# Attention stage of a fused attention and recurrent-thought kernel: VectorE normalises the results and adds five of eight causal masks, and a group's work is put in a new order

## The reference, cut to what matters

```python
xn = layernorm(x)
q, k, v = rope(xn @ wq.T), rope(xn @ wk.T), xn @ wv.T      # four query heads share one key/value head
scores = einsum(q, k) / sqrt(32) + causal_mask
attn = softmax(scores)
s = einsum(attn, v) @ wo.T
thought = layer_norm(xn)[:, -1, :] @ agg_w + agg_b
for _ in range(4):
    t = gelu(layer_norm(thought) @ d1_w + d1_b)
    thought = thought + (t @ d2_w + d2_b)
g = silu(layer_norm(xn + sigmoid(xn @ gate_w + gate_b) * (thought @ bc_w + bc_b)))
out = x + s * g
```

## Time and profile before

| | |
|---|---|
| median of 3 runs | 2551.06 us (2550.72 to 2552.27) |
| profiled execution, its own time | 2551.3 us |
| its span | 2549.6 us |
| PE busy | 2477.5 us, 97% |
| DVE busy | 1687.1 us, 66% |
| POOL busy | 1368.7 us, 54% |
| ACT busy | 981.7 us, 39% |

### The profile page before, as it was taken

How to read it: one execution, slowest core, us unless ns; L and a number is a source line. 1 busy time by engine, 2 the same in 40 slices (tenths; PEclk the granted TensorE clock), 3 DMA queues, 4 the chain that set the end, 5 groups by cost and what they waited for, 6 DMA issues and landing times. The chain is left out here.

```text
span 2549.6 us, 43562 instructions
## 1 busy us (share of the span) xinstructions
PE 2477.5 (97%) x14180; PEld 1679.2 (66%) x14180; DVE 1687.1 (66%) x3459; ACT 981.7 (39%) x1649; POOL 1368.7 (54%) x641
## 2 busy tenths in 40 slices
PE   5999999998999999999999999999899999999998
PEld 4888888885555555555555555555478888888886
DVE  5445554544777776777677777777477777777777
ACT  2111111110666665666666666666511111111111
POOL 0122212113999999999999999999511111111111
PEclk9999999997999999999999999999999999999999
DMA  6444454556755665556556656654666666655666
GB/s 247 178 151 150 161 184 175 187 172 225 208 179 168 194 207 171 179 192 205 158 189 202 181 167 195 207 176 142 237 138 124 123 123 123 123 116 114 116 117 121
DMA packets 228018, 428.90 MB, mean 168 GB/s; under 512 B 16837, under 2 KB 99781, under 8 KB 227929
## 3 DMA queue, kind: packets, MB, share of 16 engines
q1 hardware_dynamic: 154536, 375.85, 44.7%
q0 software_dynamic: 73392, 51.91, 13.9%
HBM read 313.67 MB, written 113.51 MB: 168 GB/s over the span
## 5 line engine op out<-in xcount | busy, mean ns | idle before, releaser
L961 DVE CUSTOM_DVE_ANT_0 bcast<-mxp,mask_q 128x128 f32<-128x128 f32 (+7 forms) x1024 | 726.4, 753 | 308.1 <-PE mxp L1073 175.1
L879 ACT ACTIVATE pr<-stp 128x512 f32<-128x512 f32 x1152 | 649.4, 595 | 447.3 <-PE stp L1082 332.2
L823 POOL TENSOR_TENSOR acc<-acc,pr 128x2048 f32<-128x2048 f32 x96 | 440.9, 4593 | 4.4 <-POOL acc L823 3.8
L1454 PE MATMUL gp<-g,shared 128*128 128x512 f32 x1536 | 356.1, 391 | 10.9 <-DVE g L1392 8.2
L1454 PEld LDWEIGHTS gp<-g,shared 128*128 128x128 f32 x1536 | 290.0, 189 | 72.0 <-DVE g L1392 8.5
L1454 PE MATMUL op<-o,shared 128*128 128x512 f32 x1280 | 311.2, 389 | 3.2 <-DVE shared L1442 3.2
L1094 PE MATMUL yp<-pr,vs 128*32 128x512 f32 (+3 forms) x3088 | 306.8, 492 | 0.0
L1454 PEld LDWEIGHTS op<-o,shared 128*128 128x128 f32 x1280 | 240.2, 188 | 53.9 <-DVE shared L1442 4.0
L322 POOL TENSOR_TENSOR r<-rt,r 128x1024 fp32r<-128x1024 f32 x40 | 95.9, 2397 | 279.7 <-ACT r L357 279.7
L1082 PE MATMUL stp<-qs,shared 97*128 97x512 f32 x576 | 238.6, 453 | 3.3 <-ACT pr L879 2.7
L1082 PE MATMUL stp<-shared 97*128 97x512 f32 x576 | 238.7, 452 | 0.0
(11 more groups left out here) (169 smaller groups left out, 3574.9 us busy)
## 6 DMA issues: line engine op xcount, KB each, us to landing
wch<-in_d_w SPq DMA_DIRECT2D x132, 1024.0 KB, 9.7
shared<-xt_scratch POOLq DMA_DIRECT2D x66, 512.0 KB, 6.3
q_scratch<-r SPq DMA_DIRECT2D x64, 512.0 KB, 3.6
shared<-q_scratch SPq DMA_DIRECT2D x96, 256.0 KB, 8.2
qs<-q_scratch SPq DMA_DIRECT2D x96, 256.0 KB, 7.9
yr<-y_scratch POOLq DMA_DIRECT2D x33, 512.0 KB, 5.9
xs<-in_x SPq DMA_DIRECT2D x33, 512.0 KB, 5.5
y_scratch<-ys SPq DMA_DIRECT2D x65, 256.0 KB, 2.1
```

The costliest lines, as they stand in the source:

```text
L823: nc.gpsimd.tensor_tensor(acc[:], other, pr[1][:, :, at:at + HALF], ALU.add).then_inc(add_done, 1)
L879: nc.scalar.activation(pr[half][:, :, at:at + P], stp[u % 2][:].rearrange("p (h t) -> p h t", h=REP), ACT.Exp, scale=SCALE).then_inc(act_d ...
L961: last = nc.vector.tensor_tensor_reduce(out=bcast[:, k % 2, hh * step:hh * step + w], in0=mxp[k % 2][:, hh * step + c0:hh * step + c0 + w] ...
L1454: last = nc.tensor.matmul(bank[:, cols], lhs[pa][:, k, :], ws[pw][k][:, cols], start=(k == 0 and (pa, pw) == (0, 0)), stop=(k == KT - 1 an ...
```

## The change

It has four parts, all in the attention phase.

1. **Normalisation.** `rinv` is gone. The transpose that spreads the inverse sums writes back into the PSUM bank `trp`, and VectorE itself multiplies `ys` by it (one 128x512 operation for each half, two for each group). `trp` is now freed behind this multiplication, no longer behind the first transpose. GpSimd's `normalise` is gone.
2. **Masks.** For units 4, 26, 30, 33 and 35 there is no mask matmul. VectorE adds `mask_k` to the scores in their PSUM bank (`dm`, a 128x512 operation), and ScalarE's exponential waits for that. Units 0, 7 and 9 keep the matmul.
3. **Order.** The plan is new. `fa` and `fb` are split in two parts each, with other work between; `ss 1` goes from slot 19 to slot 26; `pv 1 0` to `pv 1 3` and `ss 0` stand together in slot 28.
4. The use numbers of `trp` follow the new order.

```diff
-3: mx 20, mx 21
...
-19: ss 1
...
+0: fa 0, mx 20
+2: mx 21, fa 1, fc
...
+26: dm 26, ss 1, rc 1
+27: mx 13, mx 14
+28: pv 1 0, pv 1 1, ss 0, pv 1 2, pv 1 3
+29: rc 0
+30: dm 30, mx 15, mx 16
+31: mt 0, pv 1 4, gb, gs
+33: dm 33, mx 17, mx 18, pk 0, pk 1
+34: pv 1 5
+35: dm 35, mx 19, pk 2, pk 3
...
+DVE_MASKED = [e[1] for slot in PLAN for e in slot if e[0] == "dm"]
+PE_MASKED = [u for u, (_, j, i) in enumerate(ST) if i == j and u not in DVE_MASKED]
...
-            def normalise(half, n):
-                pool.wait_ge(ys_done, 2 * n + 3 - half)
-                pool.wait_ge(rc_done, 2 * n + 2 - half)
-                nc.gpsimd.tensor_tensor(ys[half][:], ys[half][:], rinv[half][:], ALU.mult).then_inc(yn_done, 1)
...
-                    act.wait_ge(st_done, NST * n + u + 2)
+                    if u in DVE_MASKED:
+                        act.wait_ge(dm_done, len(DVE_MASKED) * n + DVE_MASKED.index(u) + 1)
+                    else:
+                        act.wait_ge(st_done, NST * n + u + 2)
...
-                nc.vector.transpose(sq_t[:].rearrange("p a u -> p (a u)"), trp[:]).then_inc(tr_free, 1)
-                dve.wait_ge(tr_free, tu + 2)
+                nc.vector.transpose(sq_t[:].rearrange("p a u -> p (a u)"), trp[:]).then_inc(tq_done, 1)
+                dve.wait_ge(tq_done, 2 * k + 2 - half)
                 nc.vector.reciprocal(rr[half][:], sq_t[:, :, 0]).then_inc(rr_done, 1)
-                dve.wait_ge(yn_done, 2 * k + 2 - half)
                 dve.wait_ge(rr_done, 2 * k + 2 - half)
-                nc.vector.transpose(rinv[half][:], rr[half][:].unsqueeze(2).to_broadcast([P, SPREAD, SQUARE])
+                nc.vector.transpose(trp[:], rr[half][:].unsqueeze(2).to_broadcast([P, SPREAD, SQUARE])
                                     ).then_inc(rc_done, 1)
+                dve.wait_ge(ys_done, 2 * k + 3 - half)
+                dve.wait_ge(rc_done, 2 * k + 2 - half)
+                nc.vector.tensor_tensor(ys[half][:], ys[half][:], trp[:], ALU.mult).then_inc(yn_done, 1)
+                dve.wait_ge(yn_done, 2 * k + 4 - half)
+                dve.sem_inc(tr_free, 1)
...
+                        elif e[0] == "dm":
+                            bank = stp[e[1] % 2][:].rearrange("p (h t) -> p h t", h=REP)
+                            dve.wait_ge(st_done, NST * n + e[1] + 2)
+                            nc.vector.tensor_tensor(bank, bank, mask_k[:].unsqueeze(1).to_broadcast([P, REP, P]),
+                                                    ALU.add).then_inc(dm_done, 1)
...
-                if i == j:
+                if u in PE_MASKED:
                     last = nc.tensor.matmul(bank, ident16[:], mask_k[:].unsqueeze(1).to_broadcast([P, REP, P]),
                                             start=False, stop=True)
```

More of the change, by code:

```diff
@@ L68 @@
 PLAN_TEXT = """
-1: fa 0, fa 1
-2: fc
-3: mx 20, mx 21
[L72 to L83, removed]
-19: ss 1
[L85 to L96, removed]
+0: fa 0, mx 20
+2: mx 21, fa 1, fc
+4: pv 1 6, pv 1 7
+5: mt 1, dm 4, mx 0
+6: cy 1, mx 1
+7: fb 0
+9: mx 2, mx 3
+11: fb 1
+13: mx 4, mx 5
+15: pv 0 0
+16: fs
+17: mx 6, mx 7
+18: pv 0 1
+20: mx 8, mx 9
+21: ft
+22: mx 10, ls
+23: mx 11, l0, lc
+24: pv 0 2, pv 0 3, cy 0, mx 12, ga, gc, lq
+25: ge, l1, lv
+26: dm 26, ss 1, rc 1
[7 more added lines that the diff above has]
+35: dm 35, mx 19, pk 2, pk 3
 """
@@ L568, in attention_phase @@
         rr = [sb(f"rr{i}", [P, SPREAD], F32) for i in range(2)]
-        rinv = [sb(f"rinv{i}", [P, HALF], F32) for i in range(2)]
         ys = [sb(f"ys{i}", [P, HALF], F32) for i in range(2)]
@@ L601, in attention_phase @@
         y_out = [sem(f"a_y_out{i}") for i in range(2)]
-        rr_done, rc_done, yn_done = sem("a_rr"), sem("a_rc"), sem("a_yn")
+        tq_done, rr_done, rc_done, yn_done = sem("a_tq"), sem("a_rr"), sem("a_rc"), sem("a_yn")
         b1_in, c_in = sem("a_b1_in"), sem("a_c_in")
@@ L607, in attention_phase @@
         st_done, act_done, add_done, add0_done = sem("a_st"), sem("a_act"), sem("a_add"), sem("a_add0")
+        dm_done = sem("a_dm")
         mx_done, mx_free = sem("a_mx"), sem("a_mx_free")
@@ L627, in attention_phase @@
         uses = [{"fa": 0, ("mt", 1): 1, "fb": 2, "ft": 3, ("ss", 1): 4, ("ss", 0): 5, ("mt", 0): 6},
-                {"fa": 0, ("mt", 1): 1, "fb": 2, "ft": 3, ("ss", 1): 4, "l0": 5, ("ss", 0): 6, "l1": 7, ("mt", 0): 8},
-                {"fa": 0, ("mt", 1): 1, "fb": 2, "ft": 3, ("ss", 1): 4, ("ss", 0): 5, "ga": 6, "gb": 7}]
+                {"fa": 0, ("mt", 1): 1, "fb": 2, "ft": 3, "l0": 4, "l1": 5, ("ss", 1): 6, ("ss", 0): 7, ("mt", 0): 8},
+                {"fa": 0, ("mt", 1): 1, "fb": 2, "ft": 3, "ga": 4, ("ss", 1): 5, ("ss", 0): 6, "gb": 7}]
         def turns(engine, turn):
@@ L823, in turn @@
                     nc.gpsimd.tensor_tensor(acc[:], other, pr[1][:, :, at:at + HALF], ALU.add).then_inc(add_done, 1)
-                    if j == 1:
-                        normalise(1, n)
                     if j == 2:
-                        normalise(0, n)
                         if "l1" in use:
@@ L835, in _ @@
             turns(pool, turn)
-            normalise(1, GROUPS)
             pool.wait_ge(x0_in, 32)
@@ L1082, in scores @@
                 last = nc.tensor.matmul(bank, ks[par][:, j * P:(j + 1) * P], qs[par][:, i // 4, :, (i % 4) * P:(i % 4 + 1) * P],
-                                        start=True, stop=i != j)
-                if i == j:
+                                        start=True, stop=u not in PE_MASKED)
+                if u in PE_MASKED:
                     last = nc.tensor.matmul(bank, ident16[:], mask_k[:].unsqueeze(1).to_broadcast([P, REP, P]),
```

## The result

The changed kernel takes 2612.5 us (median of 4 runs, 2607.1 to 2616.3) beside 2551.7 for the kernel before: a ratio of 1.0239, interval [1.0218, 1.0259]. The forecast was 2562 with a range of 2540 to 2580. The sign was right. The size was not: the loss is 61 us, and the prediction had found 11 of them.

What follows compares the result with a forecast made beforehand. TensorE's stream was taken as the bound. Masks -1.17, order +0.60 and waits +0.95 gave +0.38 us a group, +11.8 over 31 groups, less 0.6 at the end: from 2551.3 to 2562 us, range 2540 to 2580.

Steps and rivals of the forecast that it cites:

- The chain on VectorE from mask 26 to mask 30: VectorE's run of masks, normalisations and row maxima late in a group, said to make TensorE wait 0.48 us at unit 32.
- the prices of writes to PSUM: VectorE operations writing PSUM cost the same as neighbouring rows; 0 extra taken, between -0.15 and +0.15 us each.
- the waits at the end of the group: TensorE waits for late VectorE work: 0.48 us at unit 32, 0.25 at unit 33, 0.22 at `mx 18`.
- The sum: Net effect on each attention group from masks, order and waits: +0.38 us, for 31 groups.
- Masks: Five mask matmuls fewer on TensorE, 0.235 us each: -1.17 us a group.
- The order: The new plan has 14 fp32 stretches on TensorE, not 12, at 0.3 us each: +0.60 us a group.
- The normalisation with its waits: VectorE, also normalising, is late behind mask 26, so TensorE waits late in the group: +0.95 us a group.
- At the very end a 1.29 us multiplication becomes 0.69: -0.6: After the last group the normalising multiplication gets shorter on VectorE, saving 0.6 us once.
- The layer norm moves with its own waits, three groups of 32: The layer norm's move in the plan, in three of 32 groups, was listed among covered edits, at nothing.
- The granted clock is 1.00: TensorE's granted clock in one attention group, read from the trace of the kernel before.
- waits at other units such as 6 or 1: Sign that would prove the forecast wrong: TensorE waiting in a group elsewhere than behind slot 31.
- every VectorE mask stalls: Rival: PSUM writes cost twice the fixed part, masks 33 and 35 late too; +1.0 us or more, 2583 up; chance 0.11.

Runs made afterwards that it cites:

- e3: The changed kernel with the normalisation back on GpSimd, five masks still on VectorE and the new order kept; 2563.5 us, ratio 1.0044.
- e12: e9 with mask 30 back on TensorE as a matmul; 2553.7 us, ratio 1.0011.
- e9: The changed kernel with VectorE's loop over the batches written out and the layer-norm sums ahead of row maxima 10 and 12; 2567.4 us, ratio 1.0061.
- e4: The changed kernel with only the new order left: masks back on TensorE, normalisation back on GpSimd; 2578.0 us, ratio 1.0103.
- e8: The changed kernel with normalisation back on GpSimd, VectorE's loop written out and the layer-norm sums ahead of the row maxima; 2541.5 us, ratio 0.9964.
- e6: The changed kernel with the two layer-norm sums moved ahead of row maxima 10 and 12; 2597.2 us, ratio 1.0185.
- e5: The changed kernel with only VectorE's loop over the batches written out; 2580.3 us, ratio 1.0117.
- e7: The kernel before with 26 instructions that do no work (increments of an unused semaphore) added to VectorE's loop body; 2586.9 us, ratio 1.0146.
- e2: The changed kernel with all masks back on TensorE, normalisation on VectorE and the new order kept; 2585.9 us, ratio 1.0132.

## Why the prediction was right in sign and wrong in size

**The steps that held.** The chain on VectorE from mask 26 to mask 30 (8.09 forecast, 8.21 measured), the prices of writes to PSUM, and the waits at the end of the group. By the starts of the scores, the changed kernel falls behind e3 by 0.59 us at unit 32, 0.15 at unit 33 and 0.27 at unit 34, and by no more than 0.03 before; forecast were 0.48, 0.25 and 0.22. The view of waits lists only about 0.3 of it. e12 took away 0.43 us for a forecast of 0.50. The sum was +0.38 us a group; e9 has +0.34. The changed kernel itself has +0.54: VectorE's loop makes the chain 0.15 longer (8.20 against 8.05), which is most of the difference and has no term in the sum. So e9's closeness is in part luck, as the next paragraph shows too.

**The terms that were off, with opposite signs.** Masks: -1.17 forecast, -0.86 measured (e4 to e3), 0.17 each and not 0.235. The order: +0.60 forecast, +0.43 measured. The normalisation with its waits: +0.95 forecast, +0.97 measured (e3 to after), +0.85 where VectorE's loop is written out (e8 to e9). "At the very end a 1.29 us multiplication becomes 0.69: -0.6" had the wrong sign. From the last group's first scores to the first output product it takes 56.8 us before and 61.7 in e9. TensorE waits there 4.0 us, not 1.2, for VectorE's `fsb`, a row of the recurrence's last step that only this group has; e8, with the normalisation on GpSimd, needs 58.2. From the first group's first scores to the last group's, e9 takes 9.7 us more than the kernel before (1152.1 and 1142.4). With the 4.9 at the end that is 15 us over the kernel before (16.0 by the medians, 11.2 forecast), inside the range that was given.

**The steps that failed.**

1. "The layer norm moves with its own waits, three groups of 32", entered at nothing. Its waits did not just move with it: the kernel before waits three times, 3.2 us in all and 1.1 at the longest, with no fall. In the new plan the two sums stand behind row maxima, and TensorE arrives 1.1 and 1.2 us before them. That is 7 us of waits, and the clock falls behind them. Taking these waits away was worth 15.3 us (e6).
2. VectorE's program had no term at all. I counted what its new instructions take to execute, and not that there are 30 more in a loop body. They cost little where they run. They cost 3.1 to 4.4 us of VectorE's time where the loop jumps back, since the body is then loaded again, and 1.4 to 2.7 of these reach TensorE. With the falls behind them that is 29.4 of the 32.2 us that e5 gives back.
3. "The granted clock is 1.00" was read from the trace before and taken as given. It was a property of a stream whose longest wait between 634 and 1813 us was 1.2 us. An estimate splits the 45.1 us that e9 gives back against the changed kernel: the half-clock stretches are about 58 / 2 = 29, taking half of such a stretch as lost work, and the waits themselves 11.6 + 3.4 + 3.3 = 18.3. Together that is 47, 2 more than measured.

The prediction named "waits at other units such as 6 or 1" as what would prove it wrong. They came in slot 5, ahead of `mt 1`. The rival *every VectorE mask stalls* had the right range (2583 and up) for a reason that the runs exclude.

**What stays open.** What decides whether a loop body is held. Length alone doesn't: bodies of 258 and 268 instructions were not loaded again, 278 were in the first of the four loops only (e3), 288 in the first three (the changed kernel), and 284 in all four (e7). Where the loop lies in VectorE's program seems to count. In the built program the four loops start at VectorE's instruction 432, 940, 1448 and 1956 in the changed kernel, and at 432, 944, 1456 and 1968 in e7. Divide the program into blocks of 256 instructions, with 59 more ahead of those that I can count: then each of the loops that were loaded again touches three blocks, and every other one of these kernels touches two. Both numbers are fitted to these runs, 128 and 512 fit as well as 256, and no run moved a loop without changing its length. And the first 100 us of the output phase have two or three half-clock stretches in most of these kernels, where the kernel before has one; it is worth a few us, and no run looks into it.

## What to carry to other kernels

Where one engine is busy without a gap, a wait costs its own length and may cost the clock as well: here waits of 1.1 to 2.7 us came with 3.4 to 10.2 us at half clock. So look for waits that come only in some groups (the first after a jump back, the one with extra work) before pricing the common one. When an engine's loop body grows, look at the page's instruction packets and for idle time put down to "issue" at the head of the loop; writing that engine's loop out removed it here. And two moves that each fit an engine's idle time may not fit together, as the table of e2 to e4 shows: try them apart.

## What the runs showed of the hardware

- VectorE's loop of 258 instructions is held: from group 2 to 5 the trace before has no instruction packet. With 284 or 288, each jump back that loads again brings packets of 8192 bytes and a gap of 3.1 to 4.4 us (4.6 to 5.5 in e7, where some 1.9 of it was idle before). In straight code the same packets come without a gap (e5: 50 packets, no "issue" wait on VectorE).
- TensorE's granted clock fell to 0.50, which is 1.2 GHz, from 0.2 us ahead of the end of a single wait of 1.4 to 2.7 us to 2.0 us behind it (the six groups of the changed kernel), or within 0.5 us of the start of the second of two waits, of 1.10 and 1.04 to 1.20 us. It stayed there for 3.4, 6.8 or 10.2 us. A wait's length alone doesn't decide it: e8 waits up to 1.40 us in slot 0 of groups 8, 16 and 24, e6 1.53 us in group 10 and e7 2.2 us in group 4, with no fall.
- The Trainium skill (TensorE: Matmul & The Clock Gate, A second HAM failure mode: psum-queue depth-cycling) describes a kernel whose TensorE pauses briefly and often between bursts, so that its clock swings between the two levels. The trace agrees in part: the clock swings between two levels here as well, but with a single wait or a pair of them, such as the 1.67 us at group 10, and not with frequent ones.
- A VectorE operation of 128x512 that writes PSUM lasts 0.69 to 0.73 us, one that writes SBUF 0.69 to 0.71. The row maximum that waits for the multiplication's end starts 0.38 us after it in the looped program and 0.30 in the written-out one (e9); 0.27 was the nearest row.
